# A fused two-layer RWKV and cross-attention kernel: all score, bias and decay-input products in full-array form, with new hand-written orders

## The reference, cut to what matters

```python
# both RWKV layers (C=256, EXTRA_DECAY=64)
w = time_decay + jnp.tanh(xw @ decay_w1) @ decay_w2          # xw @ decay_w1 is line 1236
# gated cross-attention (16 heads of 16 channels, no biases)
scores = jnp.einsum('bhtd,bhsd->bhts', Q, K) * scale          # softmax over s after masking
# second cross-attention with its MLP: v_b, cproj_b and proj_b are added
v = (encoder_hidden_states @ v_w + v_b)
out = out @ cproj_w + cproj_b
y = jax.nn.gelu(y @ fc_w + fc_b, approximate=True) @ proj_w + proj_b
```

## Time and profile before

| what | value |
|---|---|
| time, median of 3 runs | 1177.97 us (1177.39 to 1178.48) |
| the profiled execution's own time | 1174.9 us |
| its span, first to last instruction | 1173.0 us |
| PE busy | 1047.7 us (89% of the span) |
| DVE busy | 784.8 us (67%) |
| ACT busy | 540.0 us (46%) |
| mean granted TensorE clock | 0.962 of full speed |

### The profile page before, as it was taken

The page is one execution under the profiler, slowest core; times in us unless marked ns, Lnnn a source line. Parts: engine busy times, 40 slices in busy tenths (PEclk is TensorE's granted clock), DMA queues, the critical chain, the costliest instruction groups (busy, mean ns, idle before and its releaser), DMA issues.

```text
span 1173.0 us, 21344 instructions
## 1 busy us (share of the span) xinstructions
PE 1047.7 (89%) x8866; PEld 766.1 (65%) x8866; DVE 784.8 (67%) x1078; ACT 540.0 (46%) x1645; POOL 102.5 (9%) x100
## 2 busy tenths in 40 slices
PE   7746779988998899978999989999999999999898
PEld 5534557666676657765677666775767666776677
DVE  3697569965796589779974698747984488531320
ACT  2102326652655247432576246634663455626752
POOL 1101020100100010011100101011100100100000
PEclk9977989989999899989999989999999989999999
DMA  9200000000000010000000000001000000000000
GB/s 370 76 0 1 2 20 16 1 1 20 15 2 1 1 30 6 1 2 18 14 3 2 25 11 1 2 2 39 6 1 2 28 17 1 1 10 10 24 10 18
DMA packets 14498, 23.75 MB, mean 20 GB/s; under 512 B 3905, under 2 KB 11201, under 8 KB 13762
## 3 DMA queue, kind: packets, MB, share of 16 engines
q1 hardware_dynamic: 14402, 22.39, 5.6%
HBM read 17.13 MB, written 2.10 MB: 16 GB/s over the span
## 4 chain that ended last, share of the span: by engine, by line
PE 64%; DVE 23%; ACT 6%; issue 3%; POOL 2%; DMA 1%; SPq 0%; DVEq 0%; ACTq 0%; POOLq 0%
PE PA L1263 7%; PE PB L1297 5%; DVE S_ L562 5%; PE QA L1126 5%; PE PB L1126 5%; PE QB L1377 4%; PE QB L1085 3%; DVE A L570 3%; PE QA L1393 3%; ACT big L1000 3%; PE PA L1181 3%; PE QA L1085 3%; PE PA L1106 2%; PE QA L1116 2%; PE PA L1116 2%
## 5 line engine op out<-in xcount | busy, mean ns | idle before, releaser
L1000 ACT ACTIVATE big<-QB,nmax 128x128 f32<-128x128 f32 x512 | 181.6, 376 | 82.8 <-DVE nmax L658 82.5
L562 DVE TENSOR_TENSOR_SCAN S_<-W_,A 128x1024 f32<-128x1024 f32 x64 | 146.4, 2309 | 1.8 <-ACT A L854 1.7
L1297 PE MATMUL PB<-A,common_w 128*128 128x256 f32 x512 | 128.0, 395 | 19.3 <-DVE A L570 19.3
L1297 PEld LDWEIGHTS PB<-A,common_w 128*128 128x128 f32 x512 | 97.1, 197 | 40.7 <-DVE A L570 22.5
L658 DVE TENSOR_REDUCE nmax<-QB 128x4 f32<-128x512 f32 x128 | 86.4, 684 | 50.1 <-PE QB L1377 33.9
L448 DVE SCALAR_TENSOR_TENSOR PA<-PA,rwkv_w,SX 128x512 f32<-128x512 f32 x80 | 56.5, 752 | 81.6 <-PE PA L1181 79.4
L1000 ACT ACTIVATION_READ_ACCUMULATOR big<-QB,nmax 128x1 f32 x512 | 110.3, 215 | 0.0
L1263 PE MATMUL PA<-X,rwkv_w 128*32 128x128 f32 x3072 | 98.4, 286 | 9.2 <-DVE X L457 9.0
L1263 PEld LDWEIGHTS PA<-X,rwkv_w 128*32 128x32 f32 x3072 | 87.3, 115 | 21.7 <-DVE X L457 15.5
L1377 PE MATMUL QB<-big,QX 128*128 128x256 f32 x384 | 99.4, 382 | 0.0
L1393 PE MATMUL QA<-common_w,big 128*128 128x128 f32 x512 | 80.7, 281 | 1.9 <-ACT CN L1009 0.8
(11 more groups left out here) (192 smaller groups left out, 1806.9 us busy)
## 6 DMA issues: line engine op xcount, KB each, us to landing
rwkv_w<-in_rwkv_w SPq DMA_DIRECT2D x2, 2866.0 KB, 14.5
QX<-big SPq DMA_DIRECT2D x96, 32.0 KB, 1.9
attn_w<-in_attn_w SPq DMA_DIRECT2D x2, 1031.5 KB, 16.8
mlp_w<-in_mlp_w SPq DMA_DIRECT2D x1, 2052.0 KB, 23.6
X<-in_x SPq DMA_DIRECT2D x4, 512.0 KB, 17.2
ctx<-in_ctx SPq DMA_DIRECT2D x4, 512.0 KB, 3.8
ctx<-in_ctx_t SPq DMA_DIRECT2D x4, 512.0 KB, 3.4
out<-XT SPq DMA_DIRECT2D x4, 256.0 KB, 2.0
```

The lines of the kernel that those rows point to most:

```text
L562: last = v.tensor_tensor_scan(S_[:, d].rearrange("p k t -> p (k t)"), W_[:].rearrange("p k t -> p (k t)"), A_[c % 2][:, d].rearrange("p k ...
L1000: last = s.activation(PR[:, n % 2, j], bank(2 + n % 2)[:, j * T:(j + 1) * T], ACT.Exp, bias=nmax[:, n % 2, j:j + 1], accum_out=den[:, b, h ...
L1297: last = t.matmul(y, ident, A_[c % 2][:, :, k], start=(c % 2 == 0 and k == 0), stop=False, skip_group_check=True)
```

## The change

There are five edits.

1. The scores of b = 0 take the same path as the others: SyncE spreads b = 0 into `QX[0]` as well, so the loop of spreads runs over b = 0 to 3. The first spreads on `a_q` are now those of b = 0 and b = 1; those of b = 2 wait one by one for the scores of b = 0, those of b = 3 for the scores of b = 1. TensorE waits for the four DMAs of b = 0 before the first score product (its mask product is issued before the wait).
2. `add_bias` uses all 128 rows: `bias3` is cleared by GpSimd at the start, the three parts are put in its first three rows, and the ones are a full 128 x 128 tile.
3. The decay-input product reads 128 weight columns instead of 64, and writes 128 rows; only the first 64 are read afterwards.
4. GpSimd does one more MEMSET in its setup, and SyncE waits for it before it moves the bias parts.
5. The order strings of all four engines are new.

```diff
-        bias3 = bias3_sb[0:3]
+        bias3 = bias3_sb[:]
...
-        SPREADS = [(NB - 1) // 2, NB // 2]
+        SPREADS = [NB // 2, NB // 2]
...
                 sp.wait_ge(sem["bias_setup"], 6)
+                sp.wait_ge(sem["pool_setup"], 9)
...
-                    for b in range(1, NB):
-                        if b == 1:
+                    for b in range(NB):
+                        if b == 0:
                             sp.wait_ge(sem["a_q"], u.at("a_q", HALF))
...
                         for i in range(QUAD):
-                            if b >= 3:
+                            if b >= 2:
                                 sp.wait_ge(sem["a_s"], u.at("a_s", QUAD * (b - 2) + i + 1))
...
+                q.memset(bias3_sb[:], 0.0).then_inc(sem["pool_setup"], 1)
+                pool.wait_ge(sem["pool_setup"], 9)
...
-                    return t.matmul(o, ones[0:BIASES, :], bias_rows(k), start=False, stop=True, skip_group_check=paired)
+                    return t.matmul(o, ones[:], bias_rows(k), start=False, stop=True, skip_group_check=paired)
...
-                    dw1 = rh_(L, "dw1")
+                    dw1 = rw["dw1"][0]
                     for h in range(HALF):
                         mixed(1)(h)
-                        last = t.matmul(PA[0:DEC, 0:512], dw1[:, h], flat(X5[1])[:, h], start=(h == 0), stop=(h == 1))
+                        last = t.matmul(PA[:, 0:512], r_pack[L][:, dw1 + DEC * h:dw1 + DEC * h + P], flat(X5[1])[:, h],
+                                        start=(h == 0), stop=(h == 1))
...
-                        if b and i == 0:
-                            pe.wait_ge(q_spread[b % 2], 16 * QUAD * (u.index * SPREADS[b % 2] + (b + 1) // 2))
+                        if i == 0:
+                            pe.wait_ge(q_spread[b % 2], 16 * QUAD * (u.index * SPREADS[b % 2] + b // 2 + 1))
                         for h in range(HALF):
                             o = bank(2 + n % 2)[:, 2 * h * T:2 * (h + 1) * T]
-                            if b:
-                                last = t.matmul(o, QX[b % 2][:, i, h], K2[:, :, h, b * T:(b + 1) * T], start=False, stop=True,
-                                                skip_group_check=True)
-                            else:
-                                last = t.matmul(o, Q_[rows, h, 0:T], K2[rows, :, h, 0:T], start=False, stop=True,
-                                                tile_position=(32 * i, 0), skip_group_check=True)
+                            last = t.matmul(o, QX[b % 2][:, i, h], K2[:, :, h, b * T:(b + 1) * T], start=False, stop=True,
+                                            skip_group_check=True)
```

The new TensorE string, 828 letters as before (the strings of VectorE, ScalarE and GpSimd change in the same way and are left out):

```diff
     "TensorE":
+        "HHHHHHHHHHHHHHHHHHHHHHHRRRRHHRRRRRRRRHRRRRRHHHHHRHRHHRHHAHHAHHAHHAAAHHAAAHHAAAAAHRHAAARARRAAHARRAAAA"
+        "AHRRAAAAAARAARRRARAAAAHARRRRHHAAAAHARAAHARARAAHAHHHAHHAHAAHAAHHAHHHHAAAAAAARAAAAAARRHRAAARHAAAHRARHA"
+        "ARAAAAAHAHARAAARRRRARRRRHAAHHAHHAARHAAHARAHHAARAHHHAHAAAAAHHAHHHHAHHHHAAHHAAAAAAAARAHRRARAAAAAHHAAAH"
+        "HAARRHRHAAAARHAHRRRRARHAAAAHRRRRHHAAAAHAAARHRARAAAHHAHAHHHHHAAHAAAHRRRRAAAARAAARRRARARAARRAAAHRARRRH"
+        "HARHHAAAAHAHRHAAHAAAAARARHHAAARHAAHRAHHAAAAAARAHAHAARRRAHHAAAAAARRRAAARHHRAAHHAAAARRRAARARAAAAHRHARA"
+        "AAARRRARAHARAAAHHARHHRRHAAAHAAHAHARAHHAHAHRARHHRARHRHAAHAAHAAAAAAARRRHAAHHRAHAARARRAAAHHAAAAARAAAAAA"
+        "AARARRHAAAAARRRRRRHAAAAHAARAHHRAAAAHAHRHAHAAHHARHHARRRHHRHAHRAAAAHAHAAAAAAAAARAAAARAARRRRAAHARARAAAA"
+        "RRAHRAARHAAARHRRRRHAAAHAARRAARAHAHHAARHHARHAHAAARRARAARAAAHAHHAHHAAHAAAAAAAAAAAAAAAAAAAAHAAAAHAAHHAH"
+        "HHAAAAAAHAAAAHHAHHHAAAAAAHAH",
```

More of the change, by code:

```diff
@@ L105 @@
     "VectorE":
[L106 to L110, removed]
@@ L111 @@
-        "ARRAARRARARAARARAARARRRAAHHRRRAAARAARRRHRHAAHRRRARAARHRRRHHAAAAAAAAAAAAAAAAAAAAAHHAHAAAHHHAAAAH",
+        "HHHHHHHHHHHHAHHRRHHRRRRRRRRHRRRRHRHRRHHHRHHRRRRHRRHAAAAHHRRHAAHAAAARRRRAARHAAHRRAARRARARAHRAHAAAHRRR"
+        "AAHHARRARRARAAHHHRRAAAAHHAAHHAAAHHARRAARRRRAARAARARRAARRAHAAHRARAARRHRHAAHARHHARRRHHHRAAAHARRAHAAAHA"
+        "HAAAHHARRHHAARRRRHAAHAAHAHHRAARRAHAHAHRRRRRAAAHHRRRAAARHAHRRRARAARRRAHAAHARAAHHRRRRAAARARRAHAHRRRRAR"
+        "AAHRARRHAHARHAHARRRARAAHAHARRRRRAAHHAARAAAAHHRRAARARRRAARRRARRAARARARRAHARHAARRAHHRAHAAHHRAARRRRHHAA"
@@ L112 @@
+        "RRRRAAHHARAHRHAARHHRRRRRAAARRAARARARAHHARARRAARAHAHARAAHARRRAAHHARARRARRAAHHAARARHHRRRRHHHRRAAAHRRAA"
+        "RARARAARARARRAARRAARRARAARRRAAHHARRRRHARHAHARRARRARAAHHRRRHAAAAAAAAAAAAAAAAAAHHHAAAAAAAHHHAAAAH",
     "GpSimd":
-        "HRRHAARRHAARRHAARHRARAHRRARRHRARARHRAARRHRAHAHHA",
+        "HRRHAARRHAARRHAARHRARAHRRARRHRARAHRARARRHRAHAHHA",
     "ScalarE":
-        "HHHHHHHHHHHRRRHHHRRRRHHHHRHAHHAAAHHAAAAAAAAAARAAAAAAARAAAAAAAHAAAARAARHAARAARHAAAAAAAHHAHHHARAAHHHHA"
-        "AAAAAAAAAAAAARAAAAAAAAAAAAAARAAHARRRHAAAARAAHAAAAHHHAAHAAHHHHARHAAAAAHAAAAAAAAHAAARAAAAAAAAHARAAHAAH"
@@ L117 @@
[L117 to L120, removed]
-    "TensorE":
[L122 to L130, removed]
@@ new lines @@
+        "HHHHHHHHHHRHHRRRHRHRHRHHHHAHHAARAAHHAAAAAAAARAAAAAAAAHAAAAAAAARAAAHRAARARAHAARAAAAAAAHHHAHHAAAHHAHHR"
+        "AAAAAAAAAAAARAAAAAAAAAAAAAARAHRARHARAAHARAHAAARAHAAHAHHAAAAHHHHAAAAHAAAAAAHAAAARAAAAHAAAHAAHAAAARRAH"
+        "AHHARAARAHARAAHAAAAARHAHAAAHAAARAAAAARAAAAHRAHRAARAAHAHRAAAAAAAAHHAAHRARAAHAAHAAAAAAAARRRHHAAAAAARAA"
+        "AAAAARAAAAAAHAAAAAAAHARRRAAHRAAHAHAAAAAHARHHAARRHHRAARAAHHAAAAAAAAAAAARAHAAAAAAAAAAAARAAAHAARRARAAAH"
+        "RAAAAAAAHHHAAHHARRRAARHHAARAAHHAAAAAAAAAAARAAAAAAAAARAAARAARARAHRAAAAAAHAAHARHAARARAARAAAHAHHAAAAAAA"
@@ new lines @@
+        "AAAAAAAAAAAAAAAAHAHAHAAAAAAAAAAHAHAAAAAH",
+    "TensorE":
+        "HHHHHHHHHHHHHHHHHHHHHHHRRRRHHRRRRRRRRHRRRRRHHHHHRHRHHRHHAHHAHHAHHAAAHHAAAHHAAAAAHRHAAARARRAAHARRAAAA"
[4 more added lines that the diff above has]
+        "AAARRRARAHARAAAHHARHHRRHAAAHAAHAHARAHHAHAHRARHHRARHRHAAHAAHAAAAAAARRRHAAHHRAHAARARRAAAHHAAAAARAAAAAA"
+        "AARARRHAAAAARRRRRRHAAAAHAARAHHRAAAAHAHRHAHAAHHARHHARRRHHRHAHRAAAAHAHAAAAAAAAARAAAARAARRRRAAAHARARAAA"
+        "RRAHRAARHAAARHRRRRHAAAHAARRAARAHAHHAARHHARHAHAAARRARAARAAAHAHHAHHAAHAAAAAAAAAAAAAAAAAAAAHAAAAHAAHHAH"
+        "HHAAAAAAHAAAAHHAHHHAAAAAAHAH",
```

## The result

The changed kernel takes 1146.61 us (median, 1145.66 to 1147.45) beside 1177.76 us (1177.39 to 1178.48) for the one before in the same comparison. The ratio is 0.9735, with a 95% interval of 0.9718 to 0.9751, so 31.2 us less. Runs of one kernel differ by some us along with their mean granted clock (after: 1145.7 and 1145.8 us at 0.969, 1147.4 and 1147.5 us at 0.964 and 0.966), and a profile shows one of them.

The account below looks back on a forecast made before the run. PE was taken as the bound from 560 us on, filled before 180 us by what DVE releases. Savings -20.1, waits +6.3 and lost overlap +1.2 gave -12.6 us from 1177.97, so 1165 us, range 1151 to 1179.

Parts of the forecast that it names:

- the term for the new strings: Order strings: beyond the switches counted, nothing taken for their effect, with bounds of 5 us either way.
- lost overlap with line 1195: Where line 1195 stood beside 32-row score jobs, they shared the array; about six places, at most 1.2 us lost.
- the factor of 0.72: Share of PE's saving taken to be on the path, 0.64/0.89, applied to scores, decay input and the strings' switches.
- The bias: Layer 1 and MLPs: 32 round trips between forms at 0.30 us removed, 9.6 us, of which 9.0 on the path.
- the decay input: Decay-input product in the eight units: form switches removed, 8 x 0.32 = 2.6 us of PE time before the share.
- the scores: Scores of b = 0: 32 jobs at 0.375 us each, 12.0 us of PE time before the share.
- The price of 0.18 us for a switch: On PE, each change between product forms costs 0.18 us; 141 fewer changes save 25.4 us.
- The wait: First scores of units 4 to 7 wait for the spread DMAs: 6.3 us, bounds 0 and 16.8.
- All of it lands: Rival: PE's 25.4 us all land, DMA waits are filled, unit 6's half-speed stretch goes; 1150 us, chance 0.20.
- Slower: the waits, with the clock: Rival: layer-1 units each wait 4.2 us and the clock then halves; +7.3 us, 1185 us, chance 0.08.
- The bias edit doesn't do what it says: Rival: the bias's 0.30 us come from bf16 between f32 products and stay; 9.0 us less gain, 1174 us, chance 0.04.
- Lost packing: Rival: 32-row scores overlapped more than seen, so 128 instructions cost 20.7 us more; 1186 us, chance 0.02.

Follow-up runs that it names:

- e2: Kernel before with only the four new order strings, all products in their old forms and no spread of b = 0: 1159.57 us, ratio 0.9867.
- e8: Changed kernel with b = 0 scores over all 128 rows of Q, without spreads or their wait (output not the reference's): 1138.57 us, ratio 0.9673.
- e5: Changed kernel with b = 0 scores back in the 32-row form from Q and no spread of b = 0: 1157.73 us, ratio 0.9848.
- x1: Changed kernel with all 128 score jobs in the 32-row form from Q, without any spread: 1187.66 us, ratio 1.0095.
- e3: Changed kernel with the bias products back on 3 rows: 1154.0 us, ratio 0.9817.
- e1: Changed kernel, all edits, with the four order strings of the kernel before: 1182.17 us, ratio 1.0052.
- e9: Changed kernel with b = 0 scores over all 128 rows of Q, no spreads or wait, and the old order strings: 1167.2 us, ratio 0.991.

## Why the prediction was off, point by point

**The step that failed** is the term for the new strings, the sentence "What the new strings do beside the counts above the trace of before cannot show. I take nothing, with bounds of 5 us either way." Measured, the strings alone give 15.6 us, 1.6 of which the sum had as switches. So 14 us were missing, with 3 us either way, nearly three times the bound. The bound was taken from one wait on PE in layer 1. The gain came mostly from elsewhere: 9.8 us before unit 0's first scores, where PE is idle for 55 of 181 us and, as the prediction itself said of the earlier trace rows, is filled by what DVE releases. A bound for new strings should have been read from the idle they can fill, 125 us in all. Nor was it true that the trace could not show it: the collision at 160.88 us is a row of the trace of before, and the new order of VectorE parts the two. Swapping the two letters there is worth 3.2 us.

**What PE saves.** Forecast: 24 to 25 us of busy time, to 1023, of which 20.1 on the path, less 1.2 for lost overlap with line 1195. In all, PE's busy time fell by 19.9 us, to 1027.8. Without the wait the edits give 22.8 us (e2 to e8) where the sum had 17.3 for them (20.1 less the strings' 1.6 and less the 1.2); PE's busy time falls by 23.1. By the ratios nearly all of PE's saving shows. By the spans it is 17.6 of 23.1, or 0.76, so that the factor of 0.72 for scores and decay input was too low is likely but not shown. The bias came back whole (9.7 against 9.0 on the path and 9.6 in all), the decay input is too small to tell (1.8 against 1.9), and the scores gave 11 to 21 us against 8.6. The price of 0.18 us for a switch holds: it gives 23.9 us for e2 to e8, 29.3 for e5 to x1, and 10.8 for the 60 switches of e3, where 23.1 us of busy time, 29 us and 9.7 us were measured. The Trainium skill (TensorEngine Tiling (Array Packing), Key Properties) says that a change of the tiling mode drains the engine. The starts in these traces fit that, and give it a size of 0.15 to 0.18 us; they don't show the drain itself.

**The wait.** Forecast 6.3 us: 0, 1.4, 4.2 and 0.7 in units 4 to 7. Measured 7.3, by unit 0.7, 1.9, 3.5 and 1.3. PE stood still for 10.2 us where these terms, with 4.2 for unit 4, add to 10.5. Method and sizes were right within the 3.5 us that the measurement leaves, and so was the cover in unit 4: 3.75 us of waiting there cost 0.7.

**The sum.** -15.6 (strings) - 22.8 (edits) + 7.3 (wait) = -31.1, beside the -31.2 measured. The three are steps of one path, from before by e2 and e8 to after, so they add up whatever their values; each is no surer than its two runs. The prediction's sum of -12.6 is short by 14.0 for the strings, by 5.5 for the edits, and its price of the wait was 1.0 too low (14.0 + 5.5 - 1.0 = 18.5).

**The rivals.** "All of it lands" (1150 us) came nearest, and in part by its reasons: most of PE's saving may have landed. But it had nothing for the strings, and the DMA waits were not filled. Its half-speed stretch after the first scores of unit 6 got shorter and didn't go: the mean clock from 920.5 to 930.7 us of after is 0.75, where it was 0.50. Over the whole kernel there are 18 us less at half speed (0.969 against 0.962), at most 9 us of time; by the profiles most of it comes with the edits (89 us in before, 85 in e2, 73 in e8, 71 in after). "Slower: the waits, with the clock" is what the edits do on the old strings (e1, +6.1 us, forecast +7.3), with 14.7 us of waiting on PE and a mean clock of 0.957 against 0.962. "The bias edit doesn't do what it says" and "Lost packing" are refuted by e3 and by e5 and x1: the 32-row form is the slower one.

**Still open.** Why the old strings realise only half of what the edits save: e9 gives 10.6 us where e8 gives 22.8. By the spans the two are 6.6 us (before to e9) and 17.6. PE's busy time is 1035.5 us in e9 and 1025.9 in e8. About 2 us are the 12 switches more, and the clock (0.959 against 0.968, 23 us more at half speed, much of it before unit 0's first scores) can hold the rest of the difference in busy time. Why the clock is lower there wasn't found.

## What to carry to other kernels

When a change brings a new order along with edits, the order is a term of the sum like any other: bound it by the idle of the bottleneck engine that a better order could fill, stretch by stretch, and look in the trace for small instructions with long durations beside another engine's large one. The same edits, with the wait that they add, were worth -15 us with one order and +6 us with another, so an edit is measured with the order made for it. Where a consumer needs a quarter of a transfer, let it wait for that quarter.
